# A four-layer graph network on one core: 392 indirect stores move from the stn2 sweep to the build of the stn2 table

## The chip, the cores and the metric

The kernel runs on one core of a Trainium2 chip, with the other cores idle. The metric is the device time of one execution in microseconds (us), the median of three runs. The core has five engines that take their instructions independently and wait for each other by semaphores: TensorE (PE), VectorE (DVE), ScalarE (ACT), GpSimd (POOL) and SyncE (SP). ACT, SP and POOL also issue transfers; each has a queue of its own (q10 for ACT, q1 for SP, q0 for POOL), and all three are served by the same 16 DMA engines.

## The reference

Four graph layers over 6250 nodes and 100000 edges, each followed by a residual and a layer norm. The change touches the spline layer (first) and the data of the hops (third and fourth).

```python
def spline_conv(x, row, col, basis, idx, W, b):
    z = jnp.einsum('ni,kio->nko', x, W).reshape(N * K, Fout)
    gathered = z[col[:, None] * K + idx]
    msg = jnp.einsum('es,eso->eo', basis, gathered)
    out = jax.ops.segment_sum(msg, row, num_segments=N)
    ...
h = elu(spline_conv(ones, row, col, basis, idx, stn1_w, stn1_b))
h = elu(spline_conv(h, row, col, basis, idx, stn2_w, stn2_b))     # "stn2"
h = elu(h @ stn3_w + stn3_b); t = h @ stn4_w + stn4_b
new_pseudo = clip(pseudo + t[col] - t[row], 0, 1)
...
out = spline_conv(x, row, col, basis2, idx2, conv_w, conv_b)      # "conv"
# layers 3 and 4, for each hop: summed = segment_sum(x[src], dst)
```

## The kernel before, in words

The edges are sorted by source node and laid out as 128 partitions of J = 784 edges. A spline convolution has two stages. First a table is built: for each node the products of its row with all 125 weight matrices. Then a sweep goes over the edges: each edge gathers one piece of the table (the rows around its cell), weighs it, and running sums over edges of the same node are stored.

The hops at the end of the program multiply with an adjacency matrix of counts, `adj`, in half precision in device memory. It is cleared at the start, and each edge writes a count at its own place in it: **pair scatters**. One pair scatter is one indirect transfer issued by POOL that writes 128 elements of 2 bytes, one from each partition, to 128 places. There are 784 of them, one for each column of the edge layout. `stage_pairs` computes the places (`at_a`) and the counts (`val_a`); the first reader of `adj` is the hop stage, thousands of microseconds later.

The stages around the change, in the order in which they run. Each is a block: no engine goes on to the next block until all engines have ended this one.

1. The basis sweep (the stn1 convolution needs no gathers). POOL has nothing to do there, so `scatter_pairs` (line 1134) issues the second half of the pair scatters, columns 392 to 783, one after the other, and then waits for all.
2. `stage_z` builds the table `z_stn` from `h`: 49 tiles of nodes, for each tile five planes of products (PE, line 1832), copied by DVE and ACT (line 1849) into blocks, and two stores by ACT of 2400 KB each (line 1910). After every seven tiles the node rows are turned anew (lines 1878 to 1885). Four buffers of blocks take turns, and each is filled again only when its store has landed. POOL has no instruction in this stage.
3. `spline_setup`: DVE alone computes weights and indices (lines 1616 to 1661).
4. The stn2 sweep: `stage_spline_sweep` calls `summed_sweep` with chunks of 7 columns, so 112 chunks, two to a pass of the loop, with buffers 0 and 1. For a chunk POOL waits until ACT has staged the indices (line 777, waited for at line 728) and issues seven gathers (line 731) of 128 rows of 5120 bytes each. When all seven have landed, DVE weighs and adds (lines 1952 to 1970), tells ACT that the ring buffer is free, then makes the running sums (lines 857 and 864). ACT stages the indices of the chunk after next and copies the sums out, and SP stores them (line 765, 224 KB). In the same sweep PE and ACT build the next table, `z_conv`, one tile of 112 nodes a pass, with four stores by ACT of 700 KB (line 1759): two behind a chunk of buffer 0, two behind a chunk of buffer 1.

The other half of the pair scatters, columns 0 to 391, lies in this sweep. In a chunk of buffer 0 a scatter (line 739) follows the first, third, fifth and seventh gather; in a chunk of buffer 1 it follows the first, third and fifth. That is seven in a pass, 392 in 56 passes. They take their places and counts from small buffers, `pair_at` and `pair_val`, that DVE fills at the end of each chunk (lines 829 and 830), after it has waited for the scatters of the chunk before. POOL waits for them ahead of the first scatter of a chunk (line 738).

## Time and profile before

| | us |
|---|---|
| median of 3 runs | 10564.33 |
| lowest and highest | 10558.33, 10570.27 |
| the profiled execution | 10560.79 |
| its span, first to last instruction | 10559.0 |
| table build, from its first weight product to the issue of its last store | 1950.9 to 2565.0 |
| stn2 sweep, first gather to last chunk | 2627 to about 4536 |

The trace gives, for each instruction, its engine, its line, what it writes and reads, and how long the engine sat idle before it and what ended that. For each queue it gives the packets and bytes and the time that the packets took on the 16 DMA engines. "POOLq L728" as a releaser says that POOL's own instruction stream stood at line 728, a wait, until it was let go.

### The profile page before, as it was taken

What the parts mean: (1) busy time and instruction counts of PE and PEld (TensorE: products, weight loads), DVE (VectorE), ACT (ScalarE), POOL (GpSimd) and SP (SyncE); (2) the same over time, 40 slices, a digit from 0 to 9 for tenths busy, and PEclk for the clock granted to TensorE, in tenths of its full rate; (3) what the DMA queues carried; (4) which work ended last, traced back from release to release, by engine and by line L of the source; (5) the groups of instructions that cost most, each with busy time, mean ns of one, the idle gap of its engine ahead of it and who ended that gap; (6) DMA issues with size and microseconds to landing.
All of it is one profiled execution on the core that took longest, in us unless ns stands there. A gap on an engine that the chain in (4) does not pass through costs nothing. (4 is left out here: it accounts for less than half of the span.)

```text
span 10559.0 us, 83642 instructions
## 1 busy us (share of the span) xinstructions
PE 3371.0 (32%) x18453; PEld 2152.6 (20%) x18509; DVE 5407.2 (51%) x7974; ACT 2546.2 (24%) x3836; POOL 5912.1 (56%) x6011
## 2 busy tenths in 40 slices
PE   4444200565434444354333200020000200016998
PEld 3322100343111111143332100010000200014554
DVE  5443487444666666648888322232222688873111
ACT  0222154343333333312221011110111244430000
POOL 1777577100666666656777677777776666660000
PEclk9555555787555555555555555555555555557999
DMA  8000022597999999925666211111111233336998
GB/s 330 3 3 3 15 102 93 240 387 316 365 372 371 365 368 370 370 88 161 174 174 178 51 35 38 35 33 39 35 38 37 50 97 102 102 96 201 375 394 350
DMA packets 543466, 1836.30 MB, mean 174 GB/s; under 512 B 221430, under 2 KB 283405, under 8 KB 512748
## 3 DMA queue, kind: packets, MB, share of 16 engines
q0 software_dynamic: 306640, 766.41, 24.2%
q1 hardware_dynamic: 193898, 666.86, 16.2%
q10 hardware_dynamic: 42784, 401.43, 9.1%
q8 instruction: 51, 0.84, 0.0%
q14 instruction: 93, 0.75, 0.0%
HBM read 1118.84 MB, written 715.41 MB: 174 GB/s over the span
## 5 line engine op out<-in xcount | busy, mean ns | idle before, releaser
L2470 POOL DMA_INDIRECT ring<-tab_gat,at x2352 | 2238.4, 952 | 818.8 <-issue 715.8
L731 POOL DMA_INDIRECT ring<-z_stn,at x784 | 760.6, 970 | 1254.2 <-POOLq L738 744.4
L1714 PE MATMUL pair_acc<-pair_x_w,pair_cell 32*112 32x384 f32 (+1 forms) x1120 | 779.0, 877 | 1117.6 <-PEq L1711 1117.6
L3049 PE MATMUL acc<-spot,ones 128*128 128x128 f32 x6 | 2.3, 487 | 3234.7 <-PEq L3040 3234.7
L576 POOL DMA_INDIRECT sorted<-rows,at x784 | 771.7, 984 | 457.9 <-issue 233.0
L2041 POOL DMA_INDIRECT ring<-z_conv,at x784 | 808.4, 1031 | 358.5 <-issue 237.3
L1471 PE MATMUL acc<-tile,part_rows 128*96 128x512 f16 (+3 forms) x3185 | 718.0, 375 | 152.5 <-DMA tile<-adj 100.0
L2581 DVE COPY peak<-peak 128x6 f32<-128x6 f32 x112 | 19.6, 175 | 1404.3 <-DVEq L2580 1404.3
L3049 PEld LDWEIGHTS acc<-spot,ones 128*128 128x128 f32 x6 | 1.5, 311 | 3235.4 <-issue 3235.4
L1714 PEld LDWEIGHTS pair_acc<-pair_x_w,pair_cell 32*112 32x112 f32 x1120 | 316.3, 294 | 1579.3 <-issue 1572.3
L2505 ACT ACTIVATE weights_bank<-arg 128x168 f32<-128x168 f32 (+1 forms) x112 | 31.2, 279 | 2197.7 <-ACTq L2504 2197.7
L2617 DVE TENSOR_TENSOR_SCAN sums<-decay,sums 128x1176 f32<-128x1176 f32 (+1 forms) x112 | 517.3, 4619 | 29.0 <-DVEq L2615 29.0
L739 POOL DMA_INDIRECT adj<-pair_val,pair_at x392 | 416.4, 1062 | 199.6 <-POOLq L738 100.4
L1134 POOL DMA_INDIRECT adj<-val_a,at_a x392 | 385.1, 982 | 190.2 <-issue 127.4
L2604 DVE TENSOR_TENSOR sums<-ring,weights_bank 128x1008 f32<-128x1008 f32 (+1 forms) x112 | 429.5, 3835 | 107.5 <-DVEq L2603 107.5
L1849 DVE COPY block<-planes 128x384 f32<-128x384 f32 x588 | 296.0, 552 | 337.8 <-DVEq L1868 337.8
L1471 PEld LDWEIGHTS acc<-tile,part_rows 128*96 128x96 bf16 (+1 forms) x3185 | 367.3, 125 | 486.4 <-DMA tile<-adj 177.9
L1832 PE MATMUL planes<-wsb,turned 64*128 64x384 f32 (+1 forms) x1960 | 418.2, 553 | 130.9 <-PEq L1828 122.2
L2520 ACT COPY out_rows<-sums 128x1176 f32<-128x1176 f32 (+1 forms) x112 | 442.6, 3952 | 48.9 <-ACTq L2519 48.9
L2076 PE MATMUL found<-parts,lo_rows 128*128 128x147 bf16 x2352 | 320.8, 313 | 354.9 <-PEq L2073 354.9
L1751 ACT COPY pair_block<-pair_acc 112x384 f32<-112x384 f32 (+1 forms) x896 | 380.0, 501 | 199.3 <-ACTq L1747 199.3
L864 DVE TENSOR_TENSOR_SCAN sums<-decay,sums 128x448 f32<-128x448 f32 (+1 forms) x140 | 330.9, 2363 | 36.0 <-DVEq L862 36.0
(543 smaller groups left out, 9502.5 us busy)
## 6 DMA issues: line engine op xcount, KB each, us to landing
z_stn<-block ACTq DMA_DIRECT2D x98, 2400.0 KB, 14.9
tile<-adj SPq DMA_DIRECT2D x213, 800.0 KB, 21.7
tile<-adj SPq DMA_DIRECT2D x213, 768.0 KB, 20.8
z_conv<-pair_block ACTq DMA_DIRECT2D x224, 700.0 KB, 7.7
run_gat<-out_rows SPq DMA_DIRECT2D x56, 1596.0 KB, 5.3
adj<-zero SPq DMA_DIRECT2D x49, 1568.0 KB
run_basis<-out_rows SPq DMA_DIRECT2D x28, 1750.0 KB, 5.9
ring<-tab_gat,at POOLq DMA_INDIRECT x2352
```

Of the source, the lines that this page charges most:

```text
L576: g.indirect_dma_start(out=dest, out_offset=bass.IndirectOffsetOnAxis(ap=at[b][:, k:k + 1], axis=0), in_=rows[b][:, k, :], in_offset=None) ...
L731: g.indirect_dma_start(out=view(bufs[b], k), out_offset=None, in_=table, in_offset=bass.IndirectOffsetOnAxis(ap=at[n][b][:, k:k + 1], axis ...
L739: g.indirect_dma_start(out=adj, out_offset=bass.IndirectOffsetOnAxis(ap=pair_at[b][:, k // 2:k // 2 + 1], axis=0), in_=pair_val[b][:, k // ...
L1134: g.indirect_dma_start(out=adj, out_offset=bass.IndirectOffsetOnAxis(ap=at_a[:, k:k + 1], axis=0), in_=val_a[:, k:k + 1], in_offset=None). ...
L1471: ins = pe.matmul(acc[0:w3, b, 0:c1 - c0], rows_t, ring[f % RING][:, c0:c1], start=(i == 0), stop=False)
L1714: last = pe.matmul(self.acc[g][0:self.nodes, n, 0:(hi - lo) * self.fo], self.cell[:, :], cols, start=True, stop=True)
L1832: ins = pe.matmul(self.acc[g][:, n, 0:(hi - lo) * self.fo], self.turned[rows, k, :], cols, start=True, stop=True)
L2041: g.indirect_dma_start(out=ring[b][:, k, :, :, :].rearrange("p u s o -> p (u s o)"), out_offset=None, in_=z, in_offset=bass.IndirectOffset ...
L2470: g.indirect_dma_start(out=ring[b][:, k, :], out_offset=None, in_=tab_gat, in_offset=bass.IndirectOffsetOnAxis(ap=at[b][:, k:k + 1], axis= ...
L2520: a.copy(out_rows[b][:, :, 0:n_sums], sums[b][:, :, :, :].rearrange("p h f j -> p j (h f)"))
L2604: v.tensor_tensor(sums[b][:, :, 1:per_head, :], val_of(ring[b]), ex.unsqueeze(2).to_broadcast([P, NH, width, ch]), ALU.mult)
L2617: v.tensor_tensor_scan(flat, decay[:, :, :, :].rearrange("p h f j -> p (h f j)"), flat, 0.0, ALU.mult, ALU.add).then_inc(dve_step, 1)
```

## The change

The 392 pair scatters of columns 0 to 391 leave the loop of the sweep. `stage_z` gets a block for POOL, which issues them one after the other beside the table build and waits for all of them at its end. The buffers `pair_at` and `pair_val`, DVE's filling of them and both waits go. Since `scatter_pairs` is now called twice, its semaphore is counted on from the first call.

```diff
             for k in range(first, end):
                 g.indirect_dma_start(out=adj, out_offset=bass.IndirectOffsetOnAxis(ap=at_a[:, k:k + 1], axis=0),
-                                     in_=val_a[:, k:k + 1], in_offset=None).then_inc(sem("pairs_sent"), 16)
-            g.wait_ge(sem("pairs_sent"), 16 * (end - first))
+                                     in_=val_a[:, k:k + 1], in_offset=None).then_inc(counted("pairs_sent").sem, 16)
+            sent = counted("pairs_sent")
+            sent.base += 16 * (end - first)
+            g.wait_ge(sent.sem, sent.base)
...
-        def stage_z(arr, kin, w_dram, fo, z):
+        def stage_z(arr, kin, w_dram, fo, z, pool):
...
+                @block.gpsimd
+                def _(g):
+                    pool(g)
...
-                stage_z(h1, H1, t["L0_gnn_stn2_w"], H1, z_stn2)
+                stage_z(h1, H1, t["L0_gnn_stn2_w"], H1, z_stn2, lambda g: scatter_pairs(g, at_a, val_a, 0, J // 2))
...
                     stage_spline_sweep(z_stn2, H1, cell_i, w8, keep_s, run_stn2, tail, SEVEN,
-                                       (xcur, FX, t["L0_gnn_conv_w"], FX, z_conv), (at_a, val_a))
+                                       (xcur, FX, t["L0_gnn_conv_w"], FX, z_conv))
```

POOL, one pass of the sweep's loop. Before (`ring_170` is the ring of buffer 0; that of buffer 1 follows in the same way, with three scatters):

```order
L725 UNCONDITIONAL_BRANCH
L731 DMA ring_170<-z_stn,at_181 128x1280
L739 DMA adj<-pair_val_190,pair_at_188 40339456x1
L731 DMA ring_170<-z_stn,at_181 128x1280 x2
L739 DMA adj<-pair_val_190,pair_at_188 40339456x1
L731 DMA ring_170<-z_stn,at_181 128x1280 x2
L739 DMA adj<-pair_val_190,pair_at_188 40339456x1
L731 DMA ring_170<-z_stn,at_181 128x1280 x2
L739 DMA adj<-pair_val_190,pair_at_188 40339456x1
```

POOL with the change, from the end of the block before the table build (line 893) to the end of the sweep (line 701). The second to fourth rows are the table build's block:

```order
L893 UNCONDITIONAL_BRANCH
L1940 UNCONDITIONAL_BRANCH
L1134 DMA adj<-val_a,at_a 40339456x1 x392
L1921 UNCONDITIONAL_BRANCH
L722 UNCONDITIONAL_BRANCH
L725 UNCONDITIONAL_BRANCH
L731 DMA ring_170<-z_stn,at_181 128x1280 x7
L731 DMA ring_171<-z_stn,at_182 128x1280 x7
L725 REGISTER_ALU
L725 COMPARE_AND_BRANCH
L701 UNCONDITIONAL_BRANCH
```

All 392 scatters stand in one row ahead of the sweep, and the fourteen gathers of a pass follow each other with nothing between them.

DVE, between the last work of one chunk of the sweep and the first of the next. Before:

```order
L864 SCALAR_TENSOR_TENSOR sums_183<-decay,sums_183 128x448
L869 COPY tail<-sums_183 128x64
L873 ISA
L829 ISA
L829 TENSOR_SCALAR pair_at_188<-at_a 128x4
L830 ISA
L830 COPY pair_val_190<-val_a 128x4
L1952 ISA
L1952 COPY corner_banks<-w_163 128x56
```

With the change (line 1958 is the line 1952 of before):

```order
L864 SCALAR_TENSOR_TENSOR sums_183<-decay,sums_183 128x448
L869 COPY tail<-sums_183 128x64
L1958 ISA
L1958 COPY corner_banks<-w_163 128x56
L1964 TENSOR_TENSOR corner_banks<-ring_171,corner_banks 128x7x128 x2
```

The wait for the scatters and the two small copies are gone from between the chunks.

## Rows read from the trace of the kernel before

**Rows 1.** The page, part 2: GB/s in 40 slices of 264 us.

```profile
GB/s 330 3 3 3 15 102 93 240 387 316 365 372 371 365 368 370 370 88 161 174 174 178 51 35 38 35 33 39 35 38 37 50 97 102 102 96 201 375 394 350
```

**Rows 2.** Busy time by stage: the table build, then the stn2 sweep.

```profile
core 0: us, PE busy (x) PEld busy (x) DVE busy (x) ACT busy (x) POOL busy (x), PEclk, DMA share, GB/s
1935.00:2565.00 630.00, 430.30 (x2009) 261.67 (x2009) 296.04 (x588) 276.30 (x608) 0.00 (x0) 0.86 0.89 376
2628.00:4522.00 1894.00, 776.65 (x1150) 316.65 (x1148) 1158.29 (x1665) 584.18 (x1281) 1176.41 (x1176) 0.50 0.96 368
```

**Rows 3.** Waits, sweep, 2640 to 4500: total us, times, longest.

```profile
DVE corner_banks L1952 <- DVEq L853: 510.5, 110, 17.9
POOL ring L731 <- POOLq L728: 288.6, 57, 7.1
POOL adj L739 <- POOLq L738: 99.2, 66, 1.5
```

**Rows 4.** Timeline, one pass of the sweep: start, us, engine, line [idle before].

```profile
3028.03 1.26 POOL L731 DMA_INDIRECT ring<-z_stn,at  x1 [5.69 <-POOLq L728]
3030.84 0.99 POOL L739 DMA_INDIRECT adj<-pair_val,pair_at  x1 [1.54 <-POOLq L738]
...
3032.01 0.22 DVE L1952 COPY corner_banks<-w 128x56 f32 x1 [2.15 <-DVEq L853]
3032.13 0.96 POOL L731 DMA_INDIRECT ring<-z_stn,at  x1 [0.30 <-issue]
...
3050.97 0.22 DVE L1952 COPY corner_banks<-w 128x56 f32 x1 [6.56 <-DVEq L853]
...
3060.42 0.20 ACT L777 COPY at<-cell 128x7 int32 x1 [10.36 <-ACTq L792]
3061.54 1.27 POOL L731 DMA_INDIRECT ring<-z_stn,at  x1 [4.99 <-POOLq L728]
...
3065.65 0.22 DVE L1952 COPY corner_banks<-w 128x56 f32 x1 [2.28 <-DVEq L853]
```

**Rows 5.** DMA in slices of 0.5 us, 3026 to 3046.

```profile
GB/s 430 410 410 420 410 430 297 236 205 205 379 389 393 291 11 113 113 154 399 399 369 246 287 284 348 384 397 348 297 333 371 361 392 461 394 412 433 417 397 412
```

**Rows 6.** DMA, 3046 to 3066: slices of 0.5 us, and the mean.

```profile
GB/s 440 430 410 430 369 389 376 359 404 418 453 395 453 402 445 399 428 438 425 430 420 423 397 430 400 430 430 410 441 399 430 399 440 420 318 266 205 389 399 378
DMA packets 1964, 8.06 MB, mean 403 GB/s; under 512 B 341, under 2 KB 503, under 8 KB 1964
```

**Rows 7.** DMA, table build, 2100 to 2190, slices of 2.25 us.

```profile
GB/s 410 418 410 452 478 418 413 410 410 418 435 482 435 405 410 55 0 0 0 452 486 427 410 410 410 410 410 486 461 410 405 410 410 418 452 478 418 410 410 410
```

**Rows 8.** DMA from 50 to 200: stores of zeros, 1568 KB each, alone.

```profile
DMA packets 5703, 63.53 MB, mean 424 GB/s; under 512 B 638, under 2 KB 638, under 8 KB 638
```

**Rows 9.** DMA from 209 to 227: such stores beside scatters of 32 bytes.

```profile
DMA packets 1048, 6.94 MB, mean 386 GB/s; under 512 B 499, under 2 KB 499, under 8 KB 499
...
q0 software_dynamic: 435, 0.06, 2.6%
...
sorted<-rows,at POOLq DMA_INDIRECT x14
```

**Rows 10.** DMA queues from 1800.5 to 1802, basis sweep, right behind a store.

```profile
q0 software_dynamic: 128, 0.00, 6.4%
```

**Rows 11.** DMA queue q0, sweep, 2640 to 4400: packets, MB, share of 16 engines.

```profile
q0 software_dynamic: 116330, 476.71, 72.1%
```

**Rows 12.** Line 1134 in the basis sweep: duration ns min/median/max, first and last start.

```profile
L1134 POOL DMA_INDIRECT adj<-val_a,at_a x392: 952/958/1407, 1302.5 to 1814.0; - x196
```

**Rows 13.** DMA queues from 1797 to 1800.5, inside a 1750 KB store.

```profile
q1 hardware_dynamic: 96, 1.34, 94.6%
...
adj<-val_a,at_a POOLq DMA_INDIRECT x4
```

**Rows 14.** Timeline at the end of the table build.

```profile
2565.04 0.34 ACTq L1910 DMA_DIRECT2D z_stn<-block  x1
2581.59 1.39 DVE L1616 TENSOR_SCALAR pos<-pseudo 128x2352 f32<-128x2352 f32 x1 [17.07 <-PEq L1919]
```

## The prediction

> **What bounds the kernel now.** I read the views from the outside in. The page's GB/s line [rows 1] says which stages move much data: slices 8 to 17 of 40 stand at 240 to 390 GB/s, and the table build and the stn2 sweep are in them. The busy times by stage [rows 2] then show no engine near full in either: in the table build PE has 430 of 630 us and POOL nothing; in the sweep DVE has 1158 and POOL 1176 of 1894 us. The DMA engines are at 0.89 and 0.96. So both stages hang mainly on transfers, and the question is what the remaining hundredths, and the make-up of the 0.96, are worth.
>
> The waits [rows 3] say that DVE waits for gathers before each chunk (510 us in 110 chunks), and POOL waits for free buffers (289 us) and for the staged scatters (99 us). DVE waits for gathers to land, so DVE does not set the pace; POOL waits too, so its instruction stream is not the bound all the time. One pass in order of time [rows 4] shows where it is. A pass lasts from the gather at 3028.03 to the gather at 3061.54, 33.5 us; on average it is 1894 us / 56 = 33.8 us. Buffer 1 lands just before 3032.01, buffer 0 just before 3050.97, buffer 1 again just before 3065.65. The two halves are not alike: 19.0 us up to buffer 0, 14.7 us up to buffer 1. The rate in slices [rows 5] shows why. Up to 3029 it is 410 to 430 GB/s. From 3029 to 3035 it falls to 236, 205 and even 11 GB/s, and it stands at 246 to 397 up to 3042. In [rows 6] it is at about 420 for more than ten microseconds, up to 3063, and drops again when the next pass starts.
>
> The low stretch is the start of buffer 0's gathers. The first gather is issued at 3028.03, then POOL waits 1.54 us for the staged scatter, issues it, and gets to its second gather only at 3032.13, 4.1 us later, when buffer 1 has landed and little is left in the queues. A gather is 128 x 5120 bytes = 0.655 MB, at 424 GB/s [rows 8] 1.55 us of all DMA engines. A POOL that issues gathers alone takes 0.96 + 0.30 = 1.26 us for one [rows 4], faster than they drain; with four scatters of 1.29 us and the wait of 1.54 us the seven gathers take 7 x 1.26 + 4 x 1.29 + 1.54 = 15.5 us, and they drain in 10.8 us. So in this part of a pass the issue on POOL is the bound, and in the rest the DMA engines are.
>
> **What the change takes from the sweep.** Three things, of which only two can show.
> - POOL loses 7 x 1.29 = 9.0 us of issue and about 99 / 56 = 1.8 us of wait in a pass. Off the path it is worth nothing; at the start of buffer 0 it closes the low stretch.
> - The DMA engines lose the scatters. What one costs them is the disputed price, bounded below.
> - DVE loses two small copies and a wait, about 1 us of a chunk. DVE waits for data in both halves (2.15 and 6.56 us in [rows 4]), so that is covered, and costs nothing even if half the cover is gone.
>
> What is late next in the sweep? The DMA engines. The stage moves 368 GB/s x 1894 us = 697 MB [rows 2], and that stays. At 424 GB/s [rows 8] it takes 1644 us (29.4 us a pass), a gain of 250 us. At 403 GB/s, the mean of a stretch of 20 us with one restart in it and scatters still present [rows 6], it takes 1730 us (30.9 us a pass), a gain of 164 us. Nothing else holds a pass at 30.9: POOL needs 14 x 1.26 = 17.6 us, and DVE at most 2 x 12.4 = 24.8, since a chunk runs from 3050.97 until DVE is ready for the next, 2.28 us ahead of 3065.65. The restart is covered too, though barely: buffer 0 lands at 3050.97, its indices are staged at 3060.42 and its next gather is issued at 3061.54, 10.6 us later; with about 1.6 us from issue to first data (the gather of 3032.13 shows in the slices from 3033.5 on, [rows 5]) that is 12.2 us. Meanwhile the engines have buffer 1's gathers, 10.8 us, and two stores of `z_conv` and one of sums, 1.43 + 0.23 MB or 3.9 us, together 14.7. If those stores fall into the other half, a gap of 1.4 us comes back, so I take 403 and not 424. The lower end is the case in which the low stretch stays and only the scatters' own DMA time goes: 45 us, from the price below.
>
> **What it adds to the table build.** POOL issues 392 scatters at 1.26 us = 494 us. It has no other instruction in the stage, which runs about 630 us, so it ends some 130 us before the others, and the block's end does not wait for it. The same instructions in the basis sweep had a median of 958 ns beside a busy DVE [rows 12], so their issue should not stretch.
>
> The DMA engines are the bound here: in [rows 7] the rate stays at 410 or more except for one gap of about 8 us in 90, when ACT turns the next seven tiles and the queue runs dry. What is put on the engines outside the gaps lengthens the stage. Three rows bound the price of one scatter:
> - Low end: right behind a store in the basis sweep, four scatters (128 packets) took 6.4% of 1.5 us on the 16 engines [rows 10], 0.024 us each. In all 9 us.
> - Middle: stores of zeros alone run at 424 GB/s [rows 8]; beside 14 scatters in 18 us [rows 9] the total is 386. 18 us x (1 - 386/424) = 1.61 us, or 0.115 us each. In all 45 us, and with 0.11 of the stage idle [rows 2] about 40.
> - High end: in the sweep q0 has 72.1% of 1760 us = 1269 us for 476.7 MB [rows 11]. At 424 GB/s these bytes take 1124 us; if all of the remaining 145 us belongs to the 365 scatters issued there, one costs 0.40 us. In all 157 us.
>
> I take the middle. It is the only one that measures scatters under a full queue of large stores, as here, by what the stores lose; the high end may count time in which a packet only waited for others. A wait of its own the change does not add except at the block's end, where nothing is late.
>
> **The sum.** Sweep -164, table build +40, together -124 us. The profiled execution took 10560.8 us and would take 10437. The median of the runs is 3.5 us above it, so the prediction is 10440.
>
> **The rivals.**
> - *The sweep fills up and the scatters are nearly free.* -250 + 9 = -241 us, 10323 at the extreme; the middle of this case is near 10370. For it: the plateau of about 420 with scatters in it. Against: any pass has a restart, and its margin is 2.5 us at best.
> - *Only DMA time moves.* The share of 0.96 [rows 2] is meant: the engines are really full, the low stretch is scatter packets being served, and what leaves the sweep comes back in the table build, 45 against 40 us, or 157 against 140. About 10555, between 10540 and 10580. Against it: in [rows 5] the rate at 3033 is 11 GB/s, when POOL had just issued its second gather, so there was nothing to serve.
> - *Slower: the stores starve the scatters.* Inside a store in the basis sweep no q0 packet was served for 3.5 us while POOL issued four scatters [rows 13]; they all came behind it. In the table build ACT always has a store queued, 98 in all. If only one scatter gets through per store, 98 are served and 294 are left when the last store is issued; the block's end waits for them. At 1.26 us each that is 370 us, against -164 from the sweep: +206, 10770. It decides from 630 / 392 = 1.6 us a scatter on. Against it: beside a full queue of stores 435 packets passed in 18 us [rows 9], at 32 to a scatter 13.6 of the 14 issued, one per 1.3 us. What the basis sweep shows is then a delay of some microseconds, not a rate. Rows of the stores are 19200 bytes in the table build and 12544 there, so a turn is longer; that leaves it some chance.
> - *The memory's rate is the ceiling of a sweep.* Taken that gathers cannot be served above their mean of 368 GB/s, however they are issued, the low stretch is only the price of the high one. The sweep keeps its 1894 us and the table build pays 40: 10604. Against it: [rows 6] holds about 420 for some 13 us on end, and gathers are 9.2 of the 12.5 MB of a pass. The Trainium skill, page "DMA: Bandwidth & Descriptors", section "Where 436 GB/s comes from", says that for transfers between HBM and SBUF the HBM side binds at about 358 GB/s a core. By that rule this rival would be the result. The trace does not agree: stores alone run at 424 GB/s [rows 8], with one core at work.
>
> **How the numbers follow.** Forecast (between 10390 and 10530) 0.62; sweep full and scatters free 0.16; only DMA time moves 0.10; starved scatters 0.07; ceiling 0.05. A measurement of this kernel can tell about 0.2%, 21 us, from no change. The first two are faster, and of the third a fifth: 0.80. The rest of the third is the same, 0.08. The last two are slower, 0.12. The range runs from 10370 (the middle of the second case) to 10550: it holds the whole forecast, half of the second case and some of the third, 0.62 + 0.08 + 0.06, and some of the tail between 10370 and 10323 belongs to combinations that I hold for less likely than their bounds; that is close to 8 in 10.
>
> **What would show it.** In the changed profile POOL should issue 392 scatters of about 0.96 us from the start of the stage, some 20 us ahead of its first product at 1950.9, to about 2426, and the table build should end 40 us later than now: its last store, at 2565.0 in [rows 14], comes at about 2605. DVE starts line 1616 some 17 us behind the last store; if it waits far longer, with POOL at its wait, the scatters were starved. In the sweep a pass should take 30.9 us, with two halves nearly alike, the rate should stay near 400 with no stretch at 200, and the first and second gather of buffer 0 should be 1.6 us apart. If the low stretch is still there, my reading of the issue was wrong; if it is gone but the rate stands at 370, the ceiling was right. A table build that grows by 140 us means the high price, with which the sweep must give back as much.

## The result, and the profile after

The changed kernel takes 10493.63 us (median of 4 runs, 10485.24 to 10499.12); the kernel before, run beside it, 10561.78 us (4 runs, 10558.33 to 10570.27). The ratio is 0.9934, with a 95% interval from 0.9916 to 0.9951. That is 68 us less. The forecast was 10440, about 122 us less than this median of before; the range from 10370 to 10550 holds the result.

The profiled execution took 10499.12 us, with a span of 10497.4. The GB/s line of its page answers to [rows 1]. Slices 9 and 10 lie in the table build, slices 12 to 17 in the stn2 sweep:

```profile
GB/s 332 3 3 3 15 96 98 190 354 385 315 393 388 391 391 393 392 52 173 174 176 179 33 35 37 36 31 39 38 35 37 50 103 103 101 94 218 365 395 347
```

In slices 12 to 17 the sweep stands at 388 to 393 where it stood at 365 to 372. Busy times by stage, with the columns of [rows 2]: the stage ahead of the build (two rows, in the kernel before and after, explained below), the build with scatters in it, the build when they are through, and the sweep. First the kernel before:

```profile
1895.00:1915.00 20.00, 18.06 (x146) 17.81 (x145) 4.72 (x8) 6.34 (x7) 0.00 (x0) 0.91 0.01 1
2000.00:2565.00 565.00, 387.08 (x1810) 235.14 (x1810) 268.48 (x534) 250.52 (x551) 0.00 (x0) 0.87 0.91 387
```

Then the kernel after:

```profile
1896.00:1930.00 34.00, 31.32 (x147) 31.06 (x146) 5.46 (x8) 6.34 (x7) 0.00 (x0) 0.50 0.00 1
2014.00:2482.00 468.00, 312.33 (x1397) 193.42 (x1395) 205.45 (x408) 192.64 (x423) 323.03 (x338) 0.83 0.91 357
2482.00:2616.00 134.00, 92.66 (x422) 53.36 (x419) 64.42 (x128) 59.32 (x131) 0.60 (x1) 0.87 0.94 400
2677.00:4464.00 1787.00, 780.21 (x1156) 318.54 (x1154) 1126.41 (x1443) 585.55 (x1285) 778.14 (x784) 0.50 0.99 390
```

The build runs at 357 GB/s while POOL scatters and at 400 afterwards (387 before), at a DMA share of 0.91 to 0.94: the DMA engines are as busy, and move less. The granted clock of PE is also lower there, 0.83 where it was 0.87, and no run holds it fixed. But PE is busy for 0.67 of the time (0.69 before), and if PE had become the limit, the DMA share should have fallen; it is 0.91 in both.

To compare kernels, two lengths are used below. The **build** runs from its first to its last product on PE, the **sweep** from DVE's first to its last weighing copy (line 1952 before, 1958 after). The two lengths are of one profiled execution of each kernel; the time is the median over all its runs. Where a kernel was profiled twice (e6 and e12), the sweeps differ by 2.6 us, so a few microseconds between two sweeps mean nothing. The expectations of e1 to e4 count each stage from other points, some 20 us longer: 631 and 667 us for the build, 1896 and 1787 for the sweep.

| kernel | build, us | sweep, us | time, us (runs) |
|---|---|---|---|
| before | 611.8 | 1877.8 | 10561.78 (4) |
| after | 647.9 | 1769.3 | 10493.63 (4) |
| e1_none | 609.3 | 1768.8 | 10457.02 (4) |
| e2_filler | 611.5 | 1885.6 | 10582.87 (10) |
| e3_behind | 610.6 | 1748.1 | 10449.38 (4) |
| e4_early | 648.3 | 1758.3 | 10460.97 (4) |
| e5_thin | 611.5 | 1874.7 | 10579.58 (1) |
| e6_late | 612.1 | 1750.9 | 10431.6 (1) |
| e7_thin_z | 636.5 | 1768.1 | 10482.96 (1) |
| e8_both | 612.1 | 1756.4 | 10440.47 (4) |
| e9_wait_only | 612.0 | 1784.8 | 10473.83 (1) |
| e10_one_later | 609.3 | 1752.6 | 10431.56 (1) |
| e11_seven_more | 649.9 | 1764.6 | 10477.88 (1) |
| e12_late_timed | 611.5 | 1753.5 | 10447.38 (5) |

So in the profiled executions the sweep lost 109 us (108.5) and the build gained 36. Their sum is -72, and the spans differ by 61.6. **The difference of 11 us has a cause that is not the change's, worth 14 us.** The first product of the build comes at 1950.9 before and at 1965.2 after, though nothing ahead of it differs. The two rows of 1895 and 1896 above show why. For the same 146 matmuls the granted clock was 0.91 in one execution and 0.50, the lower level of 1.2 GHz, in the other, and they took 20 and 34 us. In both PE had been idle for some 32 us and then worked without a gap; in one execution the clock rose behind the first 14 matmuls, in the other it stayed down. The late start is also in the traces of e3, e4, e5, e7 and e12, and not in those of e1, e2, e6, e8 to e11, kernels with and without scatters in the build alike. It comes and goes, and a single profiled time has to be read with it in mind; the two lengths of the table don't contain it.

The waits of the sweep, with the columns of [rows 3], from 2640 to 4500:

```profile
POOL ring L731 <- POOLq L728: 961.8, 111, 195.0
...
DVE corner_banks L1958 <- DVEq L853: 499.4, 112, 18.2
```

The wait for the staged scatters is gone and POOL waits for buffers in both halves, 111 times where it was 57. (Its longest wait, 195.0 us, is the one from the end of its scatters in the build to the first gather.) DVE waits for gathers about as long as before, 499 against 510 us, in a sweep that is 109 us shorter: its own copies and its wait at the end of a chunk went. One pass in order of time answers to [rows 4]:

```profile
3405.99 1.28 POOL L731 DMA_INDIRECT ring<-z_stn,at  x1 [8.06 <-POOLq L728]
3407.58 0.93 POOL L731 DMA_INDIRECT ring<-z_stn,at  x1 [0.31 <-issue]
...
3410.32 0.22 DVE L1958 COPY corner_banks<-w 128x56 f32 x1 [3.33 <-DVEq L853]
...
3437.49 1.28 POOL L731 DMA_INDIRECT ring<-z_stn,at  x1 [7.78 <-POOLq L728]
```

The pass takes 31.5 us, and the second gather of buffer 0 comes 1.6 us after the first, where it came after 4.1. And the rate in slices of 0.5 us from 3400 to 3420, which answers to [rows 5, 6]:

```profile
GB/s 456 405 415 448 410 420 430 415 430 410 430 410 451 410 410 369 225 246 338 389 307 205 195 266 294 357 374 410 381 318 372 317 376 412 425 422 417 425 456 399
```

Slices as low as the 11 and 113 GB/s of [rows 5] don't occur here. A low stretch, 195 to 410 from 3407.5 to 3416.5, is still there, though POOL issues a gather each 1.25 us in it. Busy times, with the columns of [rows 2], tell the two kinds of low stretch apart. Two parts of the one in [rows 5], in the kernel before:

```profile
3033.00:3035.00 2.00, 2.00 (x4) 0.87 (x3) 2.00 (x3) 1.27 (x4) 1.39 (x3) 0.50 0.57 98
3035.00:3042.00 7.00, 5.68 (x9) 2.09 (x7) 6.00 (x8) 1.87 (x5) 5.40 (x6) 0.50 0.99 345
```

And in the kernel after:

```profile
3409.00:3412.00 3.00, 1.66 (x3) 1.02 (x4) 1.54 (x3) 2.32 (x6) 2.39 (x3) 0.50 0.90 283
3412.00:3416.50 4.50, 4.50 (x8) 1.82 (x8) 4.35 (x5) 1.91 (x5) 2.11 (x3) 0.50 0.98 356
```

The part in which the DMA engines lacked work (share 0.57, 98 GB/s) is gone. What is left are parts in which they are busy (0.90 to 0.99) and move 283 to 356 GB/s; the kernel before had such a part too.

### The profile page after: what moved, and what is told of

Read it like the earlier page. It is cut to its first block and busy times, and to the rows that moved or that the text cites. A ratio compares the mean times of both kernels' runs of the same rounds, so it can differ in the third digit from the quotient of the medians.

```text
span 10497.4 us, 82513 instructions
## 1 busy us (share of the span) xinstructions
PE 3402.1 (32%) x18453; PEld 2177.4 (21%) x18509; DVE 5374.0 (51%) x7746; ACT 2546.3 (24%) x3836; POOL 5885.2 (56%) x6011
## 5 line engine op out<-in xcount | busy, mean ns | idle before, releaser
L1134 POOL DMA_INDIRECT adj<-val_a,at_a x784 | 760.5, 970 | 413.3 <-issue 288.6
L1851 ACT COPY block<-planes 128x384 f32<-128x384 f32 x588 | 263.9, 512 | 318.8 <-ACTq L1902 309.9
```

Of the source, the lines that this page charges most:

```text
L1134: g.indirect_dma_start(out=adj, out_offset=bass.IndirectOffsetOnAxis(ap=at_a[:, k:k + 1], axis=0), in_=val_a[:, k:k + 1], in_offset=None). ...
L1851: last = put(self.blocks[a][k % 2][:, lo:hi, slot, :], self.acc[(k * KD + plane) % 2][:, n, 0:(hi - lo) * self.fo].rearrange("p (u o) -> p ...
```

## Which part of a chunk the gain comes from

Three theories were to be told apart. **Issue:** what POOL did between the first gathers of a chunk let the DMA queues run dry. **DMA time:** the scatters' own packets took the time. **Room:** POOL's instruction stream had too little slack over the whole chunk.

**No scatters at all.** The kernel after, without the pool function in the build, so that these 392 scatters are left out of the program:

```diff
-                stage_z(h1, H1, t["L0_gnn_stn2_w"], H1, z_stn2, lambda g: scatter_pairs(g, at_a, val_a, 0, J // 2))
+                stage_z(h1, H1, t["L0_gnn_stn2_w"], H1, z_stn2, lambda g: None)
...
-                @block.gpsimd
-                def _(g):
-                    pool(g)
```

> Neither stage has the 392 pair scatters of columns 0 to 391 (they are left out, so half of the adjacency counts are missing). Theory 1 (two separate prices): the table build takes its 631 us of before again instead of 667, and the sweep stays at the 1787 us of after; in all about 36 us less than after, near 10455. Rival (the 36 us of the table build are the chance of one execution, and scatters beside stores are free): the build stays within 5 us of 667 and the time is that of after, near 10490.

The ratio to before is 0.9897 (0.9881 to 0.9914). The build is back at 609 us, and the sweep is that of after, 1769. So the two parts of the change are cleanly apart: 109 us of gain in one stage, and about 37 us given back in the other (10493.63 - 10457.02; the two were timed apart, and the builds, 647.9 and 609.3, say 39).

**The slots without the scatters.** The kernel before, each scatter replaced by a memset on POOL and a wait for it:

```diff
-                                        g.indirect_dma_start(
-                                            out=adj, out_offset=..., in_=..., in_offset=None).then_inc(sent[b].sem, 16)
+                                        g.memset(filler[:, :], 0.0).then_inc(pool_step, 1)
+                                        g.wait_ge(pool_step, 1)
+                                        g.sem_inc(pool_step, -1)
+                                        g.sem_inc(sent[b].sem, 16)
```

> The kernel before, with each of the 392 scatters in the sweep replaced by a fill of a small buffer on POOL that takes about as long (the scatters are left out, so half of the counts are missing); the wait for the staged buffers and DVE's copies stay. Theory A (the prediction's: what the sweep gains is mostly POOL's issue slots at the start of buffer 0): with the slots still taken the sweep keeps most of its length, 1896 us less about 45 us for the DMA time, so near 1850, and the time near 10515. Theory B (what the sweep gains is the DMA engines' time on the scatters): the sweep falls to the 1787 us of after, and the time to about 10455.

POOL at the start of buffer 0, in order of time:

```profile
3402.88 1.27 POOL L732 DMA_INDIRECT ring<-z_stn,at  x1 [4.15 <-POOLq L729]
3405.01 0.93 POOL L740 MEMSET filler<- 128x1000 f32 x1 [0.86 <-POOLq L739]
3406.83 0.94 POOL L732 DMA_INDIRECT ring<-z_stn,at  x1 [0.89 <-POOLq L742]
```

The second gather comes 3.95 us after the first, much as the 4.1 us of [rows 4]. The sweep took 1885.6 us, 8 more than with scatters, and the ratio is 1.0012 (1.0002 to 1.0021). Two things keep it from pricing the slot exactly. Its slot is longer than a scatter's, 1.8 us against 1.3. And six times in this sweep, as in the kernel after but not in the one before, POOL pauses ahead of the second gather of buffer 0, which the last section describes:

```profile
2896.40 0.94 POOL L732 DMA_INDIRECT ring<-z_stn,at  x1 [3.61 <-issue]
```

A pass with such a pause takes 35.5 to 37.4 us. The median pass takes 33.6, against 33.8 before, which over 56 passes is 11 us. So without a packet of a scatter in the sweep, and with longer slots, some 11 us are gained where the change gains 109. That leaves the DMA time theory little to explain; what the longer slots hide of it, the next run bounds.

**Thin scatters.** The same question from the other side. In the kernel before each scatter writes from 16 partitions, an eighth of its values, and the other seven eighths are left out; POOL spends 0.87 us on one, where it spent 0.99:

```diff
-                                            out=adj, out_offset=bass.IndirectOffsetOnAxis(ap=pair_at[b][:, k // 2:k // 2 + 1], axis=0),
-                                            in_=pair_val[b][:, k // 2:k // 2 + 1], in_offset=None).then_inc(sent[b].sem, 16)
+                                            out=adj, out_offset=bass.IndirectOffsetOnAxis(ap=pair_at[b][0:16, k // 2:k // 2 + 1], axis=0),
+                                            in_=pair_val[b][0:16, k // 2:k // 2 + 1], in_offset=None).then_inc(sent[b].sem, 16)
```

> The kernel before with its 392 scatters in their places, but each writes from 16 partitions instead of 128 (seven eighths of these counts are left out), so the DMA engines have an eighth of the writes and POOL nearly the same slots. Sweep of before, from its first to its last weighing: 1878 us; of after: 1769. If the slots between the gathers are the price, it stays above 1850 as long as POOL takes its 0.95 us for one; if the writes are, it falls to between 1769 and 1790.

The line of the scatters in this kernel, duration in ns as minimum, median and maximum, first and last start:

```profile
L739 POOL DMA_INDIRECT adj<-pair_val,pair_at x392: 865/867/1693, 2643.3 to 4521.5; - x196
```

The sweep took 1874.7 us, 3 less, and the median pass, as in the kernel of memsets, 33.6 us against 33.8. So seven eighths of the writes are worth 3 us by the whole sweep, and some 11 us by the pass. POOL pauses five times here, at two different places, and that tells something on the place:

```profile
2843.84 0.96 POOL L731 DMA_INDIRECT ring<-z_stn,at  x1 [2.61 <-issue]
...
3232.67 0.86 POOL L739 DMA_INDIRECT adj<-pair_val,pair_at  x1 [4.28 <-issue]
```

The first stands ahead of the second gather of buffer 0, and its pass takes 35.8 us. The other four, 3.11 to 4.28 us long, stand between the first and the second gather of buffer 1. Their passes take 32.9 to 34.1 us, as the others do. A delay early in buffer 1 costs nothing that can be seen; one early in buffer 0 is paid.

**Scatters behind the gathers.** Everything stays in the sweep, but POOL sends a chunk's scatters when its seven gathers are out:

```diff
-                                    if scatter and k % 2 == 0 and k // 2 < some[b]:
-                                        if k == 0:
-                                            g.wait_ge(sem(f"pairs_staged{b}"), 1)
-                                            g.sem_inc(sem(f"pairs_staged{b}"), -1)
+                                if scatter:
+                                    g.wait_ge(sem(f"pairs_staged{b}"), 1)
+                                    g.sem_inc(sem(f"pairs_staged{b}"), -1)
+                                    for k in range(some[b]):
...
```

> The kernel before, with the scatters still in the sweep, but behind the seven gathers of their chunk instead of between them, so that the gathers are issued 1.25 us apart and nothing waits for the staged buffers. Theory A (issue slots): the low stretch at the start of buffer 0 closes, the sweep pays only the DMA time of the scatters over after: near 1830 us, time near 10495. Theory B (DMA time): nothing is saved, the sweep stays near 1896 us and the time near 10560.

The sweep took 1748.1 us, with all 392 scatters in it, and the build kept its 611. (The issue theory had 1830 for it, since it still put some 45 us on the scatters' DMA time.) The ratio is 0.9882 (0.9866 to 0.9899), which ends below where that of the change begins. DVE's wait for gathers is the row that moved, here from 2700 to 4390:

```profile
DVE corner_banks L1952 <- DVEq L853: 359.0, 107, 4.8
POOL ring L731 <- POOLq L728: 272.9, 108, 4.9
```

So POOL had room for the scatters; only their place was wrong. A second form keeps them between gathers, but behind the 4th to 7th of buffer 0 and the 5th to 7th of buffer 1:

```diff
-                                    if scatter and k % 2 == 0 and k // 2 < some[b]:
-                                        if k == 0:
+                                    if scatter and k >= ch - some[b]:
+                                        m = k - (ch - some[b])
+                                        if m == 0:
...
```

> The kernel before, with as many scatters between the gathers, but later in the chunk: behind the fourth to seventh gather for buffer 0 and the fifth to seventh for buffer 1, so that the wait for the staged buffers (1.54 us) is over when POOL gets there. As many scatters as before stand ahead of the last gather of a chunk. If the start of a chunk is what matters (the wait and the first slots, with the queue empty), the sweep falls near the 1748 us of the run with all scatters behind the gathers, at most 1790. If any slot ahead of the last gather costs the same, only the wait is saved, and it stays above 1830.

Its sweep is 1750.9 us, the same. Slots between gathers cost nothing, then, if the first gathers are not held up.

**The wait alone, and one gather later.** Two things stood behind the first gather: the wait for the staged pair and the first scatter's slot. One kernel keeps the wait there and sends the scatters as late as in e6_late:

```diff
+                                    if scatter and k == 0:
+                                        g.wait_ge(sem(f"pairs_staged{b}"), 1)
+                                        g.sem_inc(sem(f"pairs_staged{b}"), -1)
+                                    if scatter and k >= ch - some[b]:
+                                        m = k - (ch - some[b])
...
```

> The kernel before, with the scatters of a chunk behind its last gathers as in e6_late, but POOL still waits for the staged pair behind the first gather of each chunk. Nothing is left out. The sweep (first to last weighing copy of DVE) took 1877.8 us with the scatters behind the 1st, 3rd, 5th and 7th gather and 1750.9 us with all of them late. If it is the wait of 1.54 us at the start of a chunk that lets the queue run empty, the sweep stays near 1870. If it is the first scatter's own issue slot of 1.3 us, the sweep comes out near 1750. If both add, it lies between, some 1800.

The other moves wait and scatters by one gather, behind the 2nd, 4th, 6th and 7th of buffer 0 and the 2nd, 4th and 6th of buffer 1:

```diff
-                                    if scatter and k % 2 == 0 and k // 2 < some[b]:
-                                        if k == 0:
+                                    if scatter and k in (1, 3, 5, 6)[:some[b]]:
+                                        m = (1, 3, 5, 6).index(k)
+                                        if m == 0:
...
```

> The kernel before, with the scatters of a chunk one gather later (behind the 2nd, 4th, 6th and 7th gather of buffer 0, behind the 2nd, 4th and 6th of buffer 1), wait included. The staged pair is ready by then, so the wait should shrink from 1.5 to about 0.3 us, while the slots stay spread over the chunk. If the price of 127 us in the sweep sits between the first and the second gather alone, the sweep drops to about 1750 to 1770. If it is the issue slots of the first half of the chunk, it stays above 1820.

POOL in order of time at the start of buffer 0, in the first of these kernels (wait only):

```profile
3428.63 1.27 POOL L731 DMA_INDIRECT ring<-z_stn,at  x1 [3.52 <-POOLq L728]
3431.40 0.94 POOL L731 DMA_INDIRECT ring<-z_stn,at  x1 [1.50 <-POOLq L737]
```

The same place in the second (one gather later), and then its busy times from 2677 to 4390:

```profile
3412.13 1.27 POOL L731 DMA_INDIRECT ring<-z_stn,at  x1 [4.19 <-POOLq L728]
3413.70 0.94 POOL L731 DMA_INDIRECT ring<-z_stn,at  x1 [0.30 <-issue]
3414.95 0.99 POOL L740 DMA_INDIRECT adj<-pair_val,pair_at  x1 [0.31 <-issue]
3416.24 0.96 POOL L731 DMA_INDIRECT ring<-z_stn,at  x1 [0.30 <-issue]
```

```profile
2677.00:4390.00 1713.00, 756.72 (x1086) 306.64 (x1084) 1134.45 (x1628) 565.38 (x1242) 1127.36 (x1137) 0.50 1.01 396
```

With the second gather 1.6 us behind the first, the sweep takes 1752.6 us; with 2.8 us (the wait alone) 1784.8; with 4.1 us (wait and slot, the kernel before) 1877.8. The whole gain of 125 us comes from moving the same seven scatters of a pass by at most one gather (then the wait is over too). In e10 as many scatters as before stand ahead of the last gather of a chunk, so what counts is what stands ahead of the early ones. e10 moves all the scatters of both buffers at once, so it does not show by itself that the first scatter of buffer 0 is enough; the pauses of e5 point to buffer 0. The wait costs 34 us (1784.8 - 1750.9), the slot on top of it 93. e9 came out a quarter of the way from 1750.9 to 1877.8, nearest to the case in which both add (some 1800). The price rises faster than the delay: 1.2 us more between two gathers cost 0.6 us in a pass, the next 1.3 us cost 1.7.

**Indices staged early.** The kernel after, but ACT prepares a chunk's indices when the chunk before in that buffer has landed, and POOL waits for the free buffer itself:

```diff
+                                g.wait_ge(sem(f"ring_free{b}"), 1)
+                                g.sem_inc(sem(f"ring_free{b}"), -1)
...
-                            a.wait_ge(sem(f"ring_free{b}"), 1)
-                            a.sem_inc(sem(f"ring_free{b}"), -1)
+                            a.wait_ge(sem(f"at_free{b}"), 1)
+                            a.sem_inc(sem(f"at_free{b}"), -1)
...
+                                v.sem_inc(sem(f"at_free{b}"), 1)
...
```

> The kernel after, but ACT stages the indices of a chunk as soon as the chunk before it in the same buffer has landed, and POOL itself waits for the ring buffer to be free, so that a restart comes about 0.9 us earlier. If the restart behind a freed buffer is what the sweep of after still waits for, a pass shortens by up to 1.8 us for two restarts: sweep between 1690 and 1760 us, time near 10440. If the DMA engines are full (share 0.99), nothing changes: 1787 us, time near 10490.

The sweep took 1758.3 us, 11 less than after, and the ratio to before is 0.9895 (0.9879 to 0.9912). The other 22 us of the 32 by which its span is shorter lie behind this sweep, where other sweeps use the same helper; they were not followed up. The same edit together with the scatters behind the gathers:

> The kernel before with the scatters behind the seven gathers of their chunk and, as in the run with early indices, indices staged as soon as a chunk has landed. If the two savings add, the sweep falls from 1748 us (scatters behind) by the 11 us that early indices gave, or by more, since nothing else stands between a freed buffer and its gathers: 1700 to 1738 us, time 10435 or less. If the sweep with scatters behind is already at what the DMA engines can do, it stays at 1748 and 10449.

1756.4 us, not less than e3_behind's 1748.1, and 10440.47 us in all, ratio 0.9883 (0.9867 to 0.99). The two savings don't add. That the sweep no longer waits for the restart once the first gathers are sent in time fits this, but was not tested apart.

## What the scatters cost in the build

**Thin scatters in the build.** The kernel after, with scatters of 16 partitions there, and only there; seven eighths of their values are left out:

```diff
+        def scatter_thin(g, at_a, val_a, first, end):
+
+            for k in range(first, end):
+                g.indirect_dma_start(out=adj, out_offset=bass.IndirectOffsetOnAxis(ap=at_a[0:16, k:k + 1], axis=0),
+                                     in_=val_a[0:16, k:k + 1], in_offset=None).then_inc(counted("pairs_sent").sem, 16)
...
-                stage_z(h1, H1, t["L0_gnn_stn2_w"], H1, z_stn2, lambda g: scatter_pairs(g, at_a, val_a, 0, J // 2))
+                stage_z(h1, H1, t["L0_gnn_stn2_w"], H1, z_stn2, lambda g: scatter_thin(g, at_a, val_a, 0, J // 2))
```

> The kernel after, with 392 scatters of 16 partitions instead of 128 beside the table build (seven eighths of these counts are left out). The build, from its first to its last product, took 611 us before, 647 after, 608 without scatters. If the price is that of the single writes, it falls to about 613; if it is that of each transfer's turn in the queues, it stays near 645.

The line of these scatters, and for comparison line 1134 of the kernel after, both stages that use it, which answers to [rows 12]:

```profile
L1922 POOL DMA_INDIRECT adj<-val_a,at_a x392: 831/836/884, 1945.3 to 2431.0; - x196
```

```profile
L1134 POOL DMA_INDIRECT adj<-val_a,at_a x784: 954/958/1407, 1303.3 to 2481.6; - x196
```

The build takes 636.5 us: 25 us above that of before, where full scatters add 36. So 0.063 us of a scatter's 0.092 us (36.1 / 392) stay when only an eighth of its writes is left. So some two thirds of the price come with the transfer, not with the writes. The row of after from 2100 to 2190, which answers to [rows 7], and the queues in the same stretch:

```profile
GB/s 410 418 401 350 410 410 401 350 384 393 384 342 410 401 359 401 410 392 333 401 401 384 345 418 405 393 154 209 10 0 273 410 410 342 410 367 376 350 410 410
DMA packets 4030, 32.03 MB, mean 356 GB/s; under 512 B 2360, under 2 KB 2360, under 8 KB 2360
...
q0 software_dynamic: 2152, 0.02, 1.8%
...
adj<-val_a,at_a POOLq DMA_INDIRECT x72
```

The scatters' packets have 1.8% of the engines, 1.6 us of 90, or 0.023 us for each of the 72. That is the low end of the forecast's three prices ([rows 10]). But the slices of 452 to 486 GB/s of [rows 7] are gone, and one slice in five stands at 333 to 359. The stores lose more than the scatters' packets take.

**Seven scatters more.** This kernel tells something else, the pauses of POOL described in the last section. The kernel after, with its first seven scatters issued once more:

```diff
-                stage_z(h1, H1, t["L0_gnn_stn2_w"], H1, z_stn2, lambda g: scatter_pairs(g, at_a, val_a, 0, J // 2))
+                stage_z(h1, H1, t["L0_gnn_stn2_w"], H1, z_stn2, lambda g: (scatter_pairs(g, at_a, val_a, 0, J // 2), scatter_pairs(g, at_a, val_a, 0, 7)))
```

> The kernel after, with seven scatters more beside the build of the stn2 table (the first seven pairs once more, same places and same values). In the kernel after POOL stands still for 4.3 us between the first and the second gather of buffer 0 in every eighth pass, which is every 112th transfer that it issues. If that pause comes with the count of transfers, it moves by seven, to the start of buffer 1's chunk, and stays 112 transfers apart; if it belongs to something in the pass (a buffer, an address), it stays where it was. If it costs the sweep most when the queue is short, at the start of buffer 0, the sweep gets shorter than 1769.3 us, down to 1750; if it costs the same anywhere, the sweep stays at 1769. The table build should grow by 7 x 0.1 us, which does not show.

The pauses of the sweep stayed where they were, between the first and the second gather of buffer 0 in every eighth pass, and 4.3 us long; the sweep, 1764.6 us, is within 5 us of after's. The pause was expected to move by seven if it came with the count of transfers; it did not, so it is not counted over the whole program.

**The better version, timed.** The kernel of e6_late once more:

> The kernel of e6_late once more, timed: the kernel before with the scatters of a chunk behind its last gathers (the 4th to 7th of buffer 0, the 5th to 7th of buffer 1). One look gave 10431.6 us. The sweep's 127 us less than before and no change in the table build give about 10440 us, a ratio of 0.988, some 55 us below the kernel after. If moving the scatters out of the sweep had a worth of its own, it would come out at 10490 or more.

The time is 10447.38 us (10440.89 to 10453.98), the ratio 0.9875 (0.9858 to 0.9892), with a sweep of 1753.5 and a build of 611.5 us. It beats the change by some 46 us, with all scatters left in the sweep.

## Why the prediction was right, and where its sum was off

- **The bound of the sweep was read rightly.** The forecast said that the issue on POOL at the start of buffer 0 was the bound there. The second gather now comes 1.6 us behind the first, as forecast, and e10, which brings this about and keeps every scatter in the sweep, gains 125 us there. The rivals that rested on another reading fell: the DMA time rival with e2 and e5, and the ceiling with the rate. The sweep runs at 390 GB/s in after and 396 in e10, and has slices of 420 and more. The Trainium skill, page "DMA: Bandwidth & Descriptors", section "Where 436 GB/s comes from", has the HBM side bind at about 358 GB/s for such transfers; these rows, with one core at work, don't agree with that sentence taken alone. By the section "Measured (HBM→SBUF, 128 partitions, SWDGE, issued from GpSimd)" of the same page of the Trainium skill, 358 GB/s is each core's share when both cores of a pair stream; no run here has two cores at work.
- **"Only the scatters' own DMA time goes: 45 us", as the least that the sweep gains, was too high.** The lower end of the sweep's term rested on the price from [rows 9]. Taking seven eighths of the writes away saves 3 us, or 11 by the median pass. The sweeps with all scatters moved to better places take 1748 to 1753 us, and the one without any 1769, of which some 20 are POOL's pauses, so about the same. In these sweeps a scatter costs nothing that can be seen; it had a price in the build, where ACT nearly always has a store queued.
- **The sweep's term, -164, was -109.** The step that was off is "At 403 GB/s": the rate is 390. Two things make the gap of 55 us. The low stretch did not vanish: passes take 31.5 us and not 30.9, that is 0.6 x 56 = 34 us. And POOL paused six times, below, at some 3.7 us each, 22 us; no rival had that. The forecast saw the restart as "covered too, though barely"; it is not covered. It also took the low stretch as one thing. The part near zero was the issue. In the other part, which is still there, the DMA engines are busy at 283 to 356 GB/s, so it is not a lack of issued gathers; why they move less just then stays open.
- **DVE's copies and wait are worth nothing, as forecast.** e3, e6 and e10 keep them, and their passes take 31.5 to 31.6 us, as those of after and e1 without a pause, in which DVE has none of them.
- **The build's term, +40, was +36.** The middle price of 0.115 us for a scatter (0.102 with the idle share taken off) came out at 0.092. The reasoning for it, by what stores lose and not by what q0 takes, holds: q0's own share would have given 9 us.
- **The issue in the build.** Forecast: 392 scatters from some 20 us ahead of the first product to about 2426. They run from 1945.99, 19.2 us ahead, to 2481.6. The late start of the stage accounts for 14 of these 55 us and three pauses of POOL for 42 (9.74 + 20.03 + 13.13, less the usual 0.30 of each). They end 134 us ahead of the last store at 2615.41 and cost nothing. The end of the block, which answers to [rows 14]:

```profile
2615.41 0.34 ACTq L1912 DMA_DIRECT2D z_stn<-block  x1
2631.83 1.39 DVE L1618 TENSOR_SCALAR pos<-pseudo 128x2352 f32<-128x2352 f32 x1 [16.90 <-PEq L1921]
```

DVE waits 16.9 us for it, as before. From first product to last store it was 614.1 us and is 650.2, against a forecast of 40 more. The rival of starved scatters fell with it.
- **The sum.** Forecast -124; with the terms as measured -109 + 36 = -73, and the medians show -68. The direction, the bound and the build's price were reasoned; that the range held is in part luck, since its upper end was set with the rival of DMA time in mind, and nothing in it allowed for the pauses.

## What to carry to other kernels

When one engine issues both the large transfers that a stage lives on and small side transfers, look at the moment when the queue is shortest: there even one extra instruction or a short wait between two large ones can be paid, here more than in proportion. Try first to move the small ones behind the large ones in the same stage. Moving them to another stage whose transfers are already the bound cost here a third of the gain, and the smaller edit was worth more. For the price of a small transfer under a full queue, go by what the big ones lose, not by the small one's own share of the DMA engines.

## What the runs showed that was not expected

**POOL pauses.** In the kernel after POOL stood still between two gathers without waiting for anything that the profile shows. In the pass that begins at 3437.49: the second gather with the pause ahead of it, DVE's start on the chunk, and the start of the next pass:

```profile
3443.05 0.94 POOL L731 DMA_INDIRECT ring<-z_stn,at  x1 [4.28 <-issue]
...
3461.83 0.22 DVE L1958 COPY corner_banks<-w 128x56 f32 x1 [8.46 <-DVEq L853]
...
3472.39 1.28 POOL L731 DMA_INDIRECT ring<-z_stn,at  x1 [11.29 <-POOLq L728]
```

DVE waits 8.46 us for the chunk of buffer 0, where it waited 4.95 in the pass before: the pause comes out at the other end. This pass takes 34.9 us, the one before it 31.5. The pause comes six times in the sweep, at 2930.80, 3186.80, 3443.05, 3698.81, 3954.72 and 4209.92, which is every 112 gathers. The six passes take 34.8 to 35.8 us against a median of 31.5, together 22 us, about the difference between the sweeps of after and e1 (1769) and those of e3, e6 and e10 (1748 to 1753). In the build POOL pauses too, ahead of its 114th, 227th and 340th scatter:

```profile
2098.16 0.95 POOL L1134 DMA_INDIRECT adj<-val_a,at_a  x1 [9.74 <-issue]
...
2260.51 0.96 POOL L1134 DMA_INDIRECT adj<-val_a,at_a  x1 [20.03 <-issue]
```

The third is 13.13 us long. In the basis sweep, with the same instructions, the pause ahead of the 114th is 3.02 us. With 16-partition scatters in the build the pauses come ahead of the 129th, 257th and 385th. The count starts anew with the stage (e11), and the length grows with what is queued on the DMA engines: 3 us in the basis sweep, 4.3 in a sweep of gathers, 10 to 20 behind stores of 2400 KB. That looks like POOL waiting for room that the transfers still under way hold. The Trainium skill, page "DMA: Bandwidth & Descriptors", section "Terms", says that descriptors of transfers issued by GpSimd are written to rings in SBUF; it gives no length at which such a ring is full, and no run here shows the ring. Against it stands that in the sweeps of before, e3, e6, e8, e9, e10 and e12, with more transfers in a pass, no such pause is seen. All of these have scatters of 128 partitions among the gathers or behind them. The sweeps with gathers alone (after, e1, e4, e7, e11), with memsets (e2) and with thin scatters (e5) have pauses. So in these runs the pauses come when the full scatters leave the sweep, and their 22 us are a second price of the change, beside the 36 us of the build. The cause stays open.

**A clock that differs between executions.** The stage ahead of the build ran at a granted clock of 0.91 in one execution and 0.50 in another of unchanged code, worth 14 us. The four runs of the kernel after lie in two pairs, 10485 to 10489 and 10499 us; that the clock makes this difference was not shown, since only one of them has a trace.
